# The fourth layer's score blocks: every four steps hold one block of each quarter of the keys

## What is computed

```python
energy = einsum('bhqd,bhkd->bhqk', q, k)
rel = clip(pos[:, None] - pos[None, :] + (N - 1), 0, bias_table.shape[0] - 1)
energy = energy + bias_table[rel].transpose(2, 0, 1)[None]
att = softmax(energy / (sqrt(C) * temp), axis=-1)
out = einsum('bhqk,bhkd->bhqd', att, v)
```

## Time and profile before

| | us |
|---|---|
| median of 3 runs | 2728.06 (2722.75 to 2734.43) |
| the profiled execution, its own time | 2729.14 |
| its span in the trace | 2727.3 |
| mean granted TensorE clock | 0.945 |
| PE busy | 2400.1 (88%) |
| DVE busy | 1532.3 (56%) |
| ACT busy | 1336.9 (49%) |

### The profile page before, as it was taken

The page is one execution under the profiler, slowest core; times in us unless marked ns, Lnnn a source line. Parts: engine busy times, 40 slices in busy tenths (PEclk is TensorE's granted clock), DMA queues, the critical chain, the costliest instruction groups (busy, mean ns, idle before and its releaser), DMA issues. The chain is left out here.

```text
span 2727.3 us, 45698 instructions
## 1 busy us (share of the span) xinstructions
PE 2400.1 (88%) x15607; PEld 1468.2 (54%) x15730; DVE 1532.3 (56%) x4364; ACT 1336.9 (49%) x2453; POOL 564.9 (21%) x591
## 2 busy tenths in 40 slices
PE   5898998999957999999995898889888888888987
PEld 3555554899954666666893344444443433344433
DVE  4777776111113555655432666666667767777763
ACT  3555556554443333332233455555554666666665
POOL 2544332000025654441002111111101001011100
PEclk9999999999986999999996899899998999999999
DMA  4222222677750000000562111111122011111101
GB/s 143 81 86 80 70 86 89 195 228 225 224 168 26 27 26 22 20 20 5 170 194 78 61 48 53 48 53 53 53 72 60 22 48 54 54 53 47 40 28 32
DMA packets 132374, 214.08 MB, mean 78 GB/s; under 512 B 22664, under 2 KB 91824, under 8 KB 125232
## 3 DMA queue, kind: packets, MB, share of 16 engines
q1 hardware_dynamic: 119936, 188.72, 23.0%
q0 software_dynamic: 10240, 20.99, 2.4%
q10 hardware_dynamic: 1968, 1.44, 0.2%
HBM read 158.50 MB, written 51.40 MB: 77 GB/s over the span
## 5 line engine op out<-in xcount | busy, mean ns | idle before, releaser
L558 DVE TENSOR_REDUCE arena<-bank 128x1 f32<-128x512 f32 (+4 forms) x1216 | 723.9, 615 | 410.4 <-PE bank L547 250.9
L633 ACT ACTIVATE arena<-bank 128x512 f32<-128x512 f32 x640 | 375.0, 599 | 380.1 <-PE bank L623 377.9
L541 PE MATMUL bank<-arena 125*128 125x512 bf16 (+3 forms) x1536 | 472.2, 345 | 28.1 <-DVE arena L558 12.1
L633 ACT ACTIVATE arena<-bank,inverse_scale 128x512 f32<-128x512 f32 x512 | 337.3, 688 | 202.9 <-PE bank L611 78.0
L611 PE MATMUL bank<-arena 128*128 128x512 bf16 (+3 forms) x1413 | 405.1, 331 | 31.7 <-DMA arena<-arena 19.9
L611 PEld LDWEIGHTS bank<-arena 128*128 128x128 bf16 x1536 | 140.1, 100 | 354.2 <-ACT arena L633 191.2
L648 PE MATMUL bank<-arena 128*32 128x512 f32 (+3 forms) x3072 | 327.2, 510 | 0.9 <-ACT arena L633 0.8
L962 POOL DMA_INDIRECT back_rows<-sorted_out,back_now x160 | 154.7, 967 | 517.1 <-PE bank L623 233.0
L541 PEld LDWEIGHTS bank<-arena 125*128 125x128 bf16 x1536 | 146.5, 101 | 198.0 <-DVE arena L558 96.1
L623 PE MATMUL bank<-mask_k,identb 128*128 128x256 bf16 (+1 forms) x640 | 165.2, 258 | 46.2 <-DMA arena<-arena 43.4
L1233 ACT ACTIVATE arena<-bank,arena 128x256 f32<-128x256 f32 x320 | 131.9, 471 | 147.8 <-PE bank L1283 147.8
(11 more groups left out here) (250 smaller groups left out, 3547.8 us busy)
## 6 DMA issues: line engine op xcount, KB each, us to landing
arena<-k_parts SPq DMA_DIRECT2D x48, 576.0 KB
arena<-q_parts SPq DMA_DIRECT2D x48, 576.0 KB
arena<-in_L_ffn_w SPq DMA_DIRECT2D x80, 320.0 KB, 3.6
arena<-in_L_ffn_w SPq DMA_DIRECT2D x80, 258.0 KB, 2.8
arena<-sorted_in SPq DMA_DIRECT2D x104, 128.0 KB, 2.7
sorted_out<-arena SPq DMA_DIRECT2D x104, 128.0 KB, 3.5
arena<-in_L_ffn_w SPq DMA_DIRECT2D x24, 512.0 KB, 3.7
k_parts<-arena SPq DMA_DIRECT2D x24, 384.0 KB
```

Of the source, the lines that this page charges most:

```text
L541: ins = pe.matmul(mx[:, k * w:(k + 1) * w], Qx[0:KMAX, h, q * P:(q + 1) * P], Kx[0:KMAX, h, 0:w], start=(k == 0 or not L.causal), stop=not ...
L558: ins = dve.reduce_max(L.mx[:, g % 2, q, heads[0]:heads[-1] + 1], mx[:, 0:w * len(heads) - far].rearrange("p (j k) -> p j k", k=w - far), ...
L633: act.activation(L.probs[:, n % L.PR, 0:w], st[:, 0:w], ACT.Exp, scale=L.scale).then_inc(L.st_free.sem, 1)
```

## The change

`full_score_blocks` rotates the key block by head. With `FIRST_KEYS = [0, 2, 1, 3]`, quarter `k` holds block `(0 + k) % 4` of head 0, `(2 + k) % 4` of head 1, `(1 + k) % 4` of head 2 and `(3 + k) % 4` of head 3. The attend matmuls of a quarter then come from four different key blocks, and the first of a head is told by the quarter, not by key block 0. The causal attention of the first and third layers keeps its order.

```diff
+FIRST_KEYS = [0, 2, 1, 3]
...
 def full_score_blocks():
-    return [[[(j, k, 0)] for j in range(HG)] for k in range(NT)]
+    return [[[(j, (FIRST_KEYS[j] + k) % NT, 0)] for j in range(HG)] for k in range(NT)]
...
                 ins = pe.matmul(bank[2][j * VW:(j + 1) * VW, T - w:T], copy_of(L.Vx, b)[:, kb, g * HG + j, :],
-                                L.probs[:, (n + i) % L.PR, c:c + w], start=(kb == 0),
+                                L.probs[:, (n + i) % L.PR, c:c + w], start=(kb == 0 if L.causal else k == 0),
                                 stop=(k == len(L.sub) - 1), skip_group_check=True)
```

## The result

The changed kernel took 2739.39 us (median of 7 runs, 2737.71 to 2742.99), the kernel before in the same comparison 2729.11 us (7 runs, 2722.29 to 2738.88). The ratio is 1.0045 with a 95% interval of 1.0026 to 1.0064: 10.3 us slower. That is under 0.5%, though the interval reaches past it. The profiled execution has a span of 2735.9 us, 8.6 more than before. I count the fourth layer from the start of its first exponential to the end of the span: 645.1 us before, 658.3 now. So the layer itself got 13.2 us longer. Its start lies 4.7 us earlier in this trace, in code that did not change.

A forecast was written before the change was run, and what follows sets the result against it. PE was taken to bound the kernel, stopped now and then by a DMA. Seven batches at +0.7 (+4.9), the last at -0.6 and the clock's +5.2 gave +9.5 on 2729.1, adjusted to 2737.5 us; range 2722 to 2750.

The forecast's parts named there:

- Head group 4: PE-bound, undisturbed head group of the fourth layer: next first score 0.4 us earlier, bounds -1.1 and +0.5.
- Step 8: In the undisturbed head group, step 8 comes 7.74 us after the first score in place of 6.69.
- the walk: PE's sequence in the fourth head group, stepped through with five costs and two rules: turned maxima at 11.0, send at 12.66.
- Head group 2: In 7 batches with a transfer behind it: send and landing 0.9 us later, +0.9, between 0 and +1.6.
- 0, if the backlog sets the landing: Lower bound for head group 2: no added time if the queue's backlog decides when the maxima land.
- Head group 1: PE's two waits for DVE shift and do not shrink: +0.1 us, between -1.1 and +0.6.
- Head group 3: Pays +1.05 us up to step 8, gains most back around and behind the GELUs: +0.1, between -0.3 and +0.6.
- Batch 8: Last batch, without the transfer behind head group 2: its four head groups sum to -0.6 us.
- the clock term: Longer PE waits behind head group 2 (about 4.2 us) bring low clock behind all 7: +5.2 us, between 0 and 7.7.
- Slower: PE finds the transfer late also after head groups 1, 3 and 4; 2746.7 us at 2.8 us needed; chance 0.30.
- The clock doesn't fall more often: More than the wait's length decides the clock, so the sum lacks its 5.2: 2732.3 us, chance 0.16.
- Faster: Even order removes the exponential loop's idle time, head groups 1, 3, 4 gain 0.8 to 1.1 us: 2710, chance 0.05.

The follow-up runs named there:

- with the clock kept up: Redundant matmuls ahead of PE's waits: order of before, 8 at head group 3 (2731.99 us); changed order, 12 there and 5 in head group 1 (2730.80 us).
- new_fill: Changed kernel plus 12 redundant score matmuls on PE ahead of the wait for head group 3's maxima, in 7 batches; 2737.82 us, ratio to the kernel before 1.0020.
- old_fill: Kernel before plus 8 redundant score matmuls on PE ahead of the wait for head group 3's maxima; 2731.99 us, ratio 0.9993.
- old_swapped: Kernel before with its quarters' key blocks in the order 0, 1, 3, 2; 2731.54 us, ratio 0.9990.
- bias_first: Kernel before with key blocks in the order 2, 3, 0, 1, all bias ahead of the send; 2776.09 us in its one run.
- the five kernels with the later half: Kernel before, changed kernel or order 0, 1, 3, 2, with the read-back's second half issued one head group later, some with redundant matmuls; medians 2716.99 to 2729.59 us.
- new_later_half: Changed kernel with the second half of the next batch's read-back issued one head group later; 2721.22 us, ratio to the kernel before 0.9967.

## Why the prediction was right

**The time.** 2737.5 was forecast, 2739.4 measured; +9.5 against +10.3. The forecast was made for the fourth layer, and in the trace that layer grew by 13.2; 4.7 us of it are offset by an earlier start of the layer in the profiled execution, in code that did not change. That the totals agree to 0.8 us is in part luck. The parts, for a batch of the six in the table:

- *Head group 4 (forecast -0.4, measured -0.13).* The step was mis-sized. Step 8 came 1.33 later in place of 1.05, since PE also waits at step 1 for the exponential of the last step's bank, whose 128-column bias now delays it. The turned maxima came 1.10 later, at 11.47, where the walk had 11.0, and the send 1.10 later in place of 0.9. The next first score, by its own row, came 0.18 later and not 0.4 earlier. The transfer held PE up by no more than a trace: the weights load of head group 4's first score stands idle for 0.23 to 0.27 us for a DMA in each of the 8 batches. In batch 5 it starts 2.23 us behind the send (2465.40 to 2467.63):

```profile
2467.63 0.10 PEld L612 LDWEIGHTS bank<-arena 128*128 128x128 bf16 x1 [0.24 <-DMA arena<-arena]
```

- *Head group 2 (forecast +0.9, measured +0.36; with the clock kept up +0.78, 18.51 to 19.29).* The send came 0.92 later in batch 5 (11.95 to 12.87), as forecast. From send to score it took less, 5.75 us there in place of 6.61. In this batch and in 2, 3 and 6 the send comes 10.0 to 10.4 us behind the read-back's issue, in place of 6.7 to 8.4 before, since the low clock in head group 1 held it up. That this is why it took less is not shown: batch 3, with 10.4, took 6.8. The bound "0, if the backlog sets the landing" was a part of the truth.
- *Head group 1 (forecast +0.1, measured +1.02).* Without the clock it is -0.04 (24.56 to 24.52), and in batches 4 and 7 of the changed kernel itself, where the clock stayed up, 24.50 and 24.51; so the waits shifted, as I had it. The wait for DVE even grew, from 1.62 to 1.84. What I did not have is the low clock behind DVE's wait, 1.07 a batch. My list of waits looked at the transfer alone, though the earlier trace rows showed two more waits.
- *Head group 3 (forecast +0.1, and the clock +0.75 a batch).* Without the clock +0.27 (20.13 to 20.40), the clock 1.47 - 0.66 = +0.81 (changed minus new_fill, before minus old_fill).

So the sum was right partly by luck: the clock made about 1.9 of the 2.33 a batch (1.07 + 0.81), where I had 0.75. The other four terms came to +0.46 together where I had +0.7: less in head groups 1 and 2, more in 3 and 4. With the clock kept up in both orders they come to +0.86. Batch 8, where I had -0.6, gained 2.4 for want of a low stretch.

**The reason for the clock term** was half right. It fell behind all 7 waits as forecast, in this one execution. But these waits were not 4.2 us long; in all PE waited 23.2 us for a DMA in front of its scores in place of 19.9, 3.3 for each of the seven, where I had said 29. The length did not decide it either: in old_swapped the clock stayed up behind 3.44 and fell behind 3.76, in the changed kernel it fell behind 2.90. What PE does ahead of the wait may count too; in the changed order it has 0.65 us of bias in the last quarter in place of 1.73. That is argued, no run took it apart, and the six equal waits in head group 1, four with a fall and two without, show that both together don't settle it. What does stays open. The Trainium skill, "TensorE: Matmul & The Clock Gate", in the section on HAM oscillation, says that a DMA wait in each round can throttle PE each time and costs half of the throttled time. It tells this of waits of some 3 to 5 us, so "by it all seven rounds are cold" asked more of the page than it says. That each round is followed by low clock these runs bear out for the changed order, with 7 of 7, and not for the order of before, with 3 of 7. By the half, the stretch of 3.4 us in batch 3 (2258.4 to 2261.8, granted clock 0.50) costs 1.7 us; the measured ones cost 1.6 in head group 1 (26.1 against 24.5), where PE has no slack, and 1.2 to 1.6 behind the transfer in batches 2 to 7. In batch 1 two such stretches follow one another, and head group 3 takes 22.90 against 20.39 in new_fill, 2.5 more.

**The rivals.** *Slower* did not happen: behind head group 3 a transfer with 2.2 us from send to score comes 0.24 late and no more, and the rival's point of decision, a landing from 2.6 us on, was not reached. Its mechanism costs time in bias_first alone. *The clock doesn't fall more often* is refuted. *Faster* is refuted by step 8 alone.

## What to carry to other kernels

Work that is spread evenly over an engine is not better by that alone. Ask what waits for the steps behind it. Here each order with more bias ahead of a send sent later, by 0.55 to 0.85 us for each us of bias more than in the order of before; whether that costs time depended on the other waits, for the order 0, 1, 3, 2 also sends later and costs nothing that was measured. Where the busiest engine waits, ask what its clock does afterwards; behind a wait of 1.8 us for another engine, slower matmuls cost nearly as much again in four batches of six. A few redundant matmuls into a bank that is overwritten anyway are a cheap test for that. In the changed order they were also a cure; in the order of before they gave nothing that the medians show.

## What the runs showed that I had not expected

- The clock fell behind waits of PE from 1.84 us (for DVE, batch 3 of the changed kernel) up, and stayed up behind one of 3.44 (old_swapped). Six waits of 1.84 with equal work ahead of them were followed by low clock four times. A stretch of some 3.4 us at the low level costs 1.2 to 1.6 us, whatever wait began it.
- Two halves of one read-back, issued within 3.2 us of each other, hold a 12 KB transfer on another queue: 5.7 to 7.4 us pass from its send to its use, against 2.2 to 3.7 behind head groups 3 and 4 of batches 1 to 7. With the first half alone it depends on how long ago that was issued: in batches 2 to 7 of the five kernels with the later half 4.5 to 6.2 us when the send came 6.7 to 8.7 us behind it, 2.9 to 3.7 when it came 9.8 to 10.4 behind.
- A low clock can help by accident: the stretches in head group 1 of new_later_half hold up the send until 9.8 to 10.4 us behind the read-back's issue, and head group 2 takes 15.8 to 16.5 us there against 18.3 and 19.1 in the batches without them.
- The order 0, 1, 3, 2, which sends 0.48 later, makes head groups 1 and 4 0.2 and 0.1 us shorter than the order 0, 1, 2, 3. Why was not tried.
